# Attention step of a fused transformer kernel: transposes ahead of scores on TensorE, low halves ahead of the maximum on VectorE

## Chip, core and metric

The kernel runs on one core of one Trainium2 chip. The metric is the device time of one execution in microseconds (us), as the median of several runs. TensorE multiplies matrices and transposes, VectorE and ScalarE work on the results in PSUM, GpSimd works in SBUF, and SyncE issues the DMAs. Each engine takes its instructions in the order in which they are written; engines meet at semaphores.

## What is computed

The reference is a block of three parts on x of 4 x 1024 x 256: a mixture-of-experts feed-forward, attention with a small MLP, and the same feed-forward again. The attention, on which the change bears, is:

```python
q = (_ln(x, lnq_s, lnq_b) @ Wq + bq).reshape(Bq, Sq, H, HD).transpose(0, 2, 1, 3)   # k, v alike; H=16, HD=64
scores = jnp.einsum('bhqd,bhkd->bhqk', q, k) / SMAX
mask = jnp.triu(jnp.full((Sq, Sq), -999.0, dtype=scores.dtype), k=Sq - 1)
p = jax.nn.softmax(scores + mask, axis=-1)
att = jnp.einsum('bhqk,bhkd->bhqd', p, v).transpose(0, 2, 1, 3).reshape(Bq, Sq, AHD)
h = att @ Wo + bo + x
...
x = x + 0.5 * _L0_ffn_ref(_layernorm(x, axis=-1), ...)
x = x + _L0_attn_ref(_layernorm(x, axis=-1), ...)
x = x + 0.5 * _L0_ffn_ref(_layernorm(x, axis=-1), ...)
```

Here Sq is 1024, so that each of 4 batches and 16 heads has a 1024 x 1024 matrix of scores.

## The kernel before

Each engine has one hand-written stream for each phase: feed-forward, attention, MLP with the second feed-forward. Nothing reorders it: the code's order is the engine's order. In the names of the profile, `f_` belongs to the first feed-forward, `a_` to attention, `m_` and `g_` to what follows.

Attention is a loop of 512 steps. A step k takes 128 queries of one head against all 1024 keys. Eight steps (QT) make a head, 16 (STEPS) a pair of heads, 32 (ITER) one iteration of the loop (NIT = 16 iterations). The first iteration (`first`) is written out, the next ones but the last run as a hardware loop, and a last piece (`last`) of eight steps drains what is left. Matrices whose product needs more precision are kept as a high half (rounded to the matmul's type) and a low half (the rest), in two slots of one tile. What a step holds:

- TensorE (`on_tensor`, PE): scores of step k into `a_sc` (4 matmuls of 512 columns, line 1586; two buffers, so that the write waits for the exponential of step k-2); transposes of the probabilities of step k-3 (LAG = 3) into `a_tr` (8 of 128 columns, line 1598; two parts of four, one bank each; each part waits until the low half of the same part of the step before is taken); values of an earlier block into `a_ov` (4 matmuls, line 1622); and in some steps a projection piece of a coming pair into `a_pj` (lines 1541 and 1550).
- VectorE (`on_vector`, DVE): in every fourth step half of a finished block (`a_half`, line 1489); in every eighth one element of mask (line 1495); the negated maximum of each row of scores (`a_nmax`, line 1498); the reciprocal of the sum of the step before (`a_rden`, line 1503); and the low halves of the transposes in two parts (`a_pT`, line 1509), each of which waits for ScalarE's high half of that part.
- ScalarE (`on_scalar`, ACT): in every fourth step the other half of the finished block (`a_ao`, line 1334); the high halves of the transposes, two parts (`a_pT`, line 1341); the exponential of the scores of step k with its row sum (`a_pr`, line 1347; the sum is fetched by a short instruction of its own, ACTIVATION_READ_ACCUMULATOR), which waits for the maximum of step k; and after it the copy of a projection piece out of PSUM (`a_staged`, lines 1302 and 1299).
- GpSimd (`on_gpsimd`, POOL): multiplies the probabilities of the step before by `a_rden` (line 1425), and splits projection pieces into halves (lines 1378 to 1404).

Which steps have a projection piece stands in a table (`PLAN`, and `PLAN_FIRST` for the first iteration); QK pieces leave ScalarE by line 1302, V pieces by line 1299. In an iteration of the hardware loop 8 steps have a QK piece and 4 a V piece; the first iteration has 8 and 7, the last 4 and none. So in the steps 3 to 511 there are 124 QK pieces and 61 V pieces, 63 steps with a mask, and 126 steps with a finished block (steps 11, 15, ..., 511).

Of the kernel before, what the change touches and what calls it, by code (L numbers as in the profile page):

```python
# [20 lines left out]
F32 = mybir.dt.float32  # L21
F32R = mybir.dt.float32r
U32 = mybir.dt.uint32
ALU = mybir.AluOpType
# [3 lines left out]
P = 128  # L28
# [986 lines left out]
def attention_phase(nc, turns, tag, w, zT, w_split, bias, att):  # L1015
# [12 lines left out]
    ITER = 2 * STEPS  # L1028
    NIT = B * PAIRS // 2
    LAG = 3  # L1030
    QT = S // P
    NP = 4
# [7 lines left out]
    ident, bsb = kept["ident"], kept["bias"]  # L1040
# [11 lines left out]
    pT = m.sb("pT", [P, 2, 2, QT, BT], F32R, room=rooms.wide)  # L1052
    pr = m.sb("pr", [P, NP, S], room=rooms.rows)
# [4 lines left out]
    tr = m.ps("tr", [P, 2, BT], 2)  # L1058
# [3 lines left out]
    s = {n: m.sem(n) for n in (  # L1062
        "z_in wqk_in wv_in v_in k_dup sc masked negmax exp rden normed tr tr_hi tr_lo "
        "pj staged head0_hi head1_hi head0_lo v_hi first_split split pv half ov_read att att_out").split()}
# [60 lines left out]
    def transposes_at(k, first, last):  # L1125
        return not (first and k < LAG) and not (last and k >= LAG)
# [338 lines left out]
    def on_vector(dve, ahead):  # L1465
        rest = whole.ffn["vector"](dve)

        for n, (kind, part) in enumerate(FIRST):
            if kind != "V":
                xs, hi, lo = parts_of(kind, part, n % 2, 0)  # L1470
                for x in range(2):
                    dve.wait_ge(s["head%d_hi" % x], n + 1)
                    dve.tensor_tensor(lo[x], xs[x], hi[x].bitcast(F32), ALU.subtract)\
                        .then_inc(s["first_split" if x else "head0_lo"], 1)

        def body(it, first, last):
            for k in steps(last):
                u = it * ITER + k
                v = finished_at(k, first)
                if v:  # L1480
                    _, vhead, blk, _ = v
                    dve.wait_ge(s["pv"], it * BLOCKS + blk + 1)
                    if blk % 4 == 0 and not (first and blk < 4):

                        dve.wait_ge(s["att"], it * 2 + blk // 4)
                    if blk == 0 and first:

                        dve.wait_ge(f["res_out"], NB * 16 + 16)
                    dve.tensor_copy(half[rows_of_head(vhead), blk % 2], ov[rows_of_head(1 - vhead)])\  # L1489
                        .then_inc(s["half"], 1)  # L1490
                if not last:
                    dve.wait_ge(s["sc"], u + 1)
                    if k % QT == 0:

                        dve.tensor_scalar(sc[0:1, k % 2, S - 1:S], sc[0:1, k % 2, S - 1:S], MASK, None,
                                          ALU.add).then_inc(s["masked"], 1)
                        dve.wait_ge(s["masked"], it * (ITER // QT) + k // QT + 1)
                    dve.tensor_reduce(nmax[:, k % NP:k % NP + 1], sc[:, k % 2], AX.X, ALU.max,  # L1498
                                      negate=True).then_inc(s["negmax"], 1)
                if (k == 0 and not first) or (k > 0 and not last):  # L1500
                    j = (k - 1) % NP
                    dve.wait_ge(s["exp"], u)
                    dve.reciprocal(rden[:, j:j + 1], den[:, j:j + 1]).then_inc(s["rden"], 1)  # L1503
                if transposes_at(k, first, last):
                    t = (k - LAG) % ITER
                    for part in range(2):
                        dve.wait_ge(s["tr_hi"], 2 * (u - LAG) + part + 1)
                        to = pT[:, (t // 4) % 2, :, 4 * part:4 * part + 4, (t % 4) * P:(t % 4 + 1) * P]
                        dve.tensor_tensor(to[:, 1], tr[:, part].rearrange("p (t q) -> p t q", t=4),  # L1509
                                          to[:, 0].bitcast(F32), ALU.subtract).then_inc(s["tr_lo"], 1)  # L1510
                if ends(it) and k == STEPS + 6:
                    ahead["b1"]()
                if last and 2 < k < 5:
                    ahead["att_lo"](k - 3)
                if first and k == 1:
                    rest["z_stats"]()
                if first and k == 3:
                    rest["zz_stats"]()
                if first and k == 4:
                    rest["bias"](ov)  # L1520
                if first and k in (5, 6):
                    rest["zt_lo"](k - 5, ov[:])
        over_iterations(dve, body)

    def on_tensor(pe, ahead):
# [37 lines left out]
        def body(it, first, last):  # L1563
            for k in steps(last):
                u = it * ITER + k
                slot, head, tile = k // STEPS, (k // QT) % 2, k % QT
                if not last:

                    if k % STEPS == 0:

                        pe.wait_ge(s["k_dup"], it * 64 + slot * 32 + 64)
                        if slot:
                            pe.wait_ge(s["split"], before(it, STEPS))
                        elif not first:
                            pe.wait_ge(s["split"], before(it, 0) - 3)
                        else:
                            pe.wait_ge(s["first_split"], 3)
                            pe.wait_ge(f["res"], NB * 2)
                    if first and k == 4:
                        pe.wait_ge(s["first_split"], 4)  # L1580
                    if not (first and k < 2):

                        pe.wait_ge(s["exp"], u - 1)
                    for kb in range(S // BT):
                        for a in range(2):
                            o = pe.matmul(sc[:, k % 2, kb * BT:(kb + 1) * BT],  # L1586
                                          q_s[:, slot, head, tile * P:(tile + 1) * P],
                                          k_s[:, slot, head, a, kb * BT:(kb + 1) * BT],
                                          start=(a == 0), stop=(a == 1))
                    o.then_inc(s["sc"], 1)  # L1590
                if transposes_at(k, first, last):
                    pe.wait_ge(s["normed"], u - LAG + 1)
                    for part in range(2):
                        if not (first and k == LAG):

                            pe.wait_ge(s["tr_lo"], 2 * (u - LAG) + part - 1)
                        for j in range(4):
                            o = pe.transpose(tr[:, part, j * P:(j + 1) * P],  # L1598
                                             pr[:, (k - LAG) % NP, (4 * part + j) * P:(4 * part + j + 1) * P], ident[:])
                        o.then_inc(s["tr"], 1)  # L1600
                v = values_at(k, first)
                if v and not (last and v[2] >= 0):
                    vslot, vhead, blk, q = v
# [562 lines left out]
```

## Time and profile before

| | us |
|---|---|
| median of 3 runs | 2459.19 |
| lowest, highest | 2451.25, 2463.77 |
| the profiled execution | 2457.1 |
| its span, first to last instruction | 2454.2 |
| first scores of attention to last, in the trace | 298 to 1982 |

The profile gives for each engine its busy time, then the chain that ended last, then groups of instructions with their busy time, the mean time of one, and the idle time of the engine ahead of them with what ended it. In a timeline a row is one instruction or a run of the same kind: its start, its busy time and, in brackets, how long the engine sat idle before it and for whom. Of two rows of one engine the difference of the starts is the pace at which it takes them; a matmul's own duration reaches over the start of the next, because matmuls are pipelined. The granted clock (PEclk) is the share of TensorE's 2.4 GHz that it had in a stretch: 1.00 is 2.4 GHz, 0.50 is 1.2 GHz.

### The profile page before, as it was taken

How to read it: one execution, taken by the hardware profiler on the slowest of the kernel's cores; microseconds unless marked ns; L12 is line 12 of the kernel's file. 1: busy time of each engine (PE TensorE's matmuls, PEld its weight loads, DVE VectorE, ACT ScalarE, POOL GpSimd, SP SyncE). 2: the span in 40 equal slices, each digit the busy share in tenths (PEclk: the TensorE clock that was granted, in tenths of full speed). 3: DMA queues.
4: the chain of work that ended last, by engine and by line, in shares of the span. 5: the costliest groups of instructions: out<-in, count | busy, mean ns of one | idle time of the engine just before them, and what ended most of it. 6: DMA issues, size and time to landing. Idle time of an engine off the chain costs nothing.

```text
span 2454.2 us, 46643 instructions
## 1 busy us (share of the span) xinstructions
PE 2405.0 (98%) x14568; PEld 2087.9 (85%) x14568; DVE 1862.3 (76%) x3599; ACT 1686.6 (69%) x2920; POOL 1505.2 (61%) x1536
## 2 busy tenths in 40 slices
PE   8999889999999999999999999999999999999999
PEld 7888778888888888888888888888888879988888
DVE  7777677878878788887878878788887865556665
ACT  4555577878778787777878778787877864543333
POOL 1333277787777777767777777777768754542220
PEclk9999999999999999999999999999999999999999
DMA  5422531223212132221213312132221345331111
GB/s 204 172 102 94 181 112 44 87 68 96 95 40 89 45 101 71 75 95 43 86 60 100 97 35 94 43 98 73 77 95 43 108 169 171 122 130 34 46 51 43
DMA packets 128311, 220.16 MB, mean 90 GB/s; under 512 B 6810, under 2 KB 89652, under 8 KB 119476
## 3 DMA queue, kind: packets, MB, share of 16 engines
q1 hardware_dynamic: 128180, 218.78, 27.6%
q8 instruction: 37, 0.61, 0.1%
q14 instruction: 94, 0.77, 0.1%
HBM read 114.95 MB, written 53.48 MB: 69 GB/s over the span
## 4 chain that ended last, share of the span: by engine, by line
PE 81%; DVE 8%; issue 6%; POOL 2%; ACT 2%; DMA 1%; SPq 0%; DVEq 0%; ACTq 0%; POOLq 0%
PE a_ov L1622 19%; PE a_sc L1586 18%; PE a_tr L1598 18%; PE a_pj L1541 7%; PE a_pj L1550 4%; PE g_acc L896 3%; PE g_hid L855 3%; PE f_acc L896 3%; PE f_hid L855 2%; PE m_proj L2025 1%; POOL m_zin L1877 1%; PE m_hid L2091 1%; DVE f_hp L676 1%; DVE g_hp L676 1%; PE g_aux L832 1%
## 5 line engine op out<-in xcount | busy, mean ns | idle before, releaser
L1498 DVE TENSOR_REDUCE a_nmax<-a_sc 128x1 f32<-128x1024 f32 x512 | 626.8, 1224 | 260.3 <-PE a_sc L1586 252.1
L1425 POOL TENSOR_SCALAR a_pr<-a_pr,a_rden 128x1024 f32<-128x1024 f32 x512 | 575.1, 1125 | 256.2 <-DVE a_rden L1503 185.7
L1341 ACT ACTIVATE a_pT<-a_tr 128x512 fp32r<-128x512 f32 x1024 | 559.8, 596 | 205.5 <-PE a_tr L1598 197.2
L1509 DVE TENSOR_TENSOR a_pT<-a_tr,a_pT 128x512 fp32r<-128x512 f32 x1024 | 650.1, 677 | 17.7 <-ACT a_pT L1341 17.7
L1622 PE MATMUL a_ov<-a_pT,a_v_s 128*128 128x512 f32 x2048 | 600.2, 415 | 3.1 <-DVE a_half L1489 2.0
L1347 ACT ACTIVATE a_pr<-a_sc,a_nmax 128x1024 f32<-128x1024 f32 x512 | 573.5, 1120 | 31.8 <-DVE a_nmax L1498 28.2
L1586 PE MATMUL a_sc<-a_k_s,a_q_s 128*128 128x512 f32 x2048 | 554.1, 392 | 3.4 <-DMA a_k_s<-a_k_s 3.4
L1598 PEld LDWEIGHTS a_tr<-f_ident,a_pr 128*128 128x128 f32 x4096 | 473.0, 140 | 93.6 <-DVE a_pT L1509 18.8
L1598 PE MATMUL a_tr<-f_ident,a_pr 128*128 128x128 f32 x4096 | 537.8, 273 | 9.8 <-DVE a_pT L1509 9.6
L1586 PEld LDWEIGHTS a_sc<-a_k_s,a_q_s 128*128 128x128 f32 x2048 | 380.0, 188 | 83.7 <-DMA a_k_s<-a_k_s 3.6
L1622 PEld LDWEIGHTS a_ov<-a_pT,a_v_s 128*128 128x128 f32 x2048 | 347.5, 189 | 54.3 <-issue 4.9
L1541 PE MATMUL a_pj<-a_z_s,a_wqk_s 128*128 128x512 f32 x756 | 193.6, 391 | 2.5 <-issue 2.2
L1541 PEld LDWEIGHTS a_pj<-a_z_s,a_wqk_s 128*128 128x128 f32 x756 | 141.6, 188 | 34.9 <-issue 3.3
L1302 ACT ACTIVATE a_staged<-a_pj,f_bias 128x512 f32<-128x512 f32 x126 | 86.8, 689 | 93.8 <-PE a_pj L1541 77.4
L469 ACT ACTIVATE g_act_out<-g_hid,f_b 128x512 f32<-128x512 f32 x72 | 49.6, 688 | 144.5 <-PE g_hid L855 144.5
L896 PEld LDWEIGHTS f_acc<-f_w2p,f_hp 128*128 128x128 f32 x864 | 114.0, 193 | 11.1 <-DVE f_hp L676 6.3
L469 ACT ACTIVATE f_act_out<-f_hid,f_b 128x512 f32<-128x512 f32 x72 | 49.2, 684 | 107.0 <-PE f_hid L855 107.0
L896 PE MATMUL f_acc<-f_w2p,f_hp 128*128 128x256 f32 x864 | 117.5, 286 | 4.5 <-DVE f_hp L676 3.9
L896 PEld LDWEIGHTS g_acc<-g_w2p,g_hp 128*128 128x128 f32 x864 | 112.1, 190 | 8.2 <-DVE g_hp L676 2.9
L896 PE MATMUL g_acc<-g_w2p,g_hp 128*128 128x256 f32 x864 | 115.5, 283 | 1.3 <-DVE g_hp L676 0.9
L855 PE MATMUL f_hid<-f_xT,f_w1p 128*128 128x512 f32 x432 | 115.7, 404 | 0.0
L855 PE MATMUL g_hid<-g_xT,g_w1p 128*128 128x512 f32 x432 | 113.1, 397 | 0.0
(222 smaller groups left out, 3260.0 us busy)
## 6 DMA issues: line engine op xcount, KB each, us to landing
a_z_s<-zT SPq DMA_DIRECT2D x32, 1024.0 KB, 7.8
a_k_s<-a_k_s SPq DMA_DIRECT2D x62, 512.0 KB, 5.7
a_wqk_s<-w_split SPq DMA_DIRECT2D x64, 256.0 KB, 3.2
a_v_s<-a_v_b SPq DMA_DIRECT2D x16, 1024.0 KB, 4.6
att<-a_ao SPq DMA_DIRECT2D x32, 512.0 KB, 2.9
m_in<-att SPq DMA_DIRECT2D x16, 1024.0 KB, 6.1
a_wv_s<-w_split SPq DMA_DIRECT2D x17, 512.0 KB, 3.8
zT<-f_zT SPq DMA_DIRECT2D x8, 1024.0 KB, 3.9
```

The lines of the kernel that those rows point to most:

```text
L469: act.activation(act_out[:, e % 3], hid[:, (par + e) % 2], ACT.Gelu, bias=b1[:, weights_of(e):weights_of(e) + 1]).then_inc(s["gelu"], 1)
L855: o = pe.matmul(hid[:, (par + e) % 2], w1p[:, a, (c * NE + x) * HID:(c * NE + x + 1) * HID], xT[:, par, c, b], start=(n == 0), stop=(n == 5))
L896: o = pe.matmul(acc[:, t], hp[:, e % 3, a, t * P:(t + 1) * P], w2p[:, b, x * D:(x + 1) * D], start=False, stop=(e == NE - 1 and (a, b) == ...
L1341: act.activation(pT[:, (u // 4) % 2, 0, 4 * part:4 * part + 4, (u % 4) * P:(u % 4 + 1) * P], tr[:, part].rearrange("p (t q) -> p t q", t=4 ...
L1347: act.activation(pr[:, k % NP], sc[:, k % 2], ACT.Exp, bias=nmax[:, k % NP:k % NP + 1], accum_out=den[:, k % NP:k % NP + 1]).then_inc(s["e ...
L1425: pool.tensor_scalar(pr[:, k % NP], pr[:, k % NP], rden[:, k % NP:k % NP + 1], 1.0, ALU.mult, ALU.mult).then_inc(s["normed"], 1)
L1498: dve.tensor_reduce(nmax[:, k % NP:k % NP + 1], sc[:, k % 2], AX.X, ALU.max, negate=True).then_inc(s["negmax"], 1)
L1509: dve.tensor_tensor(to[:, 1], tr[:, part].rearrange("p (t q) -> p t q", t=4), to[:, 0].bitcast(F32), ALU.subtract).then_inc(s["tr_lo"], 1)
L1541: o = pe.matmul(bank[:], wqk_s[:, "QK".index(kind), c, a], z_s[:, c * 2 + b, part], start=(i == 0), stop=(i == 5))
L1586: o = pe.matmul(sc[:, k % 2, kb * BT:(kb + 1) * BT], q_s[:, slot, head, tile * P:(tile + 1) * P], k_s[:, slot, head, a, kb * BT:(kb + 1) * ...
L1598: o = pe.transpose(tr[:, part, j * P:(j + 1) * P], pr[:, (k - LAG) % NP, (4 * part + j) * P:(4 * part + j + 1) * P], ident[:])
L1622: o = pe.matmul(ov[:], v_s[:, vslot, kt, 2 * vhead:2 * vhead + 2] .rearrange("p k f -> p (k f)"), pT[:, blk % 2, a, kt], start=(kt == 0 an ...
```

## The change

Two blocks of code move within a step; nothing is added or taken away, and ScalarE's, GpSimd's and SyncE's streams stay as they are. On TensorE the transposes of step k-3 come ahead of the scores of step k. On VectorE the low halves of those transposes come ahead of the mask, the maximum and the reciprocal, behind `a_half`.

```diff
@@ on_vector
                     dve.tensor_copy(half[rows_of_head(vhead), blk % 2], ov[rows_of_head(1 - vhead)])\
                         .then_inc(s["half"], 1)
+                if transposes_at(k, first, last):
+                    t = (k - LAG) % ITER
+                    for part in range(2):
+                        dve.wait_ge(s["tr_hi"], 2 * (u - LAG) + part + 1)
+                        to = pT[:, (t // 4) % 2, :, 4 * part:4 * part + 4, (t % 4) * P:(t % 4 + 1) * P]
+                        dve.tensor_tensor(to[:, 1], tr[:, part].rearrange("p (t q) -> p t q", t=4),
+                                          to[:, 0].bitcast(F32), ALU.subtract).then_inc(s["tr_lo"], 1)
                 if not last:
                     dve.wait_ge(s["sc"], u + 1)
...
                     dve.wait_ge(s["exp"], u)
                     dve.reciprocal(rden[:, j:j + 1], den[:, j:j + 1]).then_inc(s["rden"], 1)
-                if transposes_at(k, first, last):
...
@@ on_tensor
                 slot, head, tile = k // STEPS, (k // QT) % 2, k % QT
+                if transposes_at(k, first, last):
+                    pe.wait_ge(s["normed"], u - LAG + 1)
+                    for part in range(2):
+                        if not (first and k == LAG):
+
+                            pe.wait_ge(s["tr_lo"], 2 * (u - LAG) + part - 1)
+                        for j in range(4):
+                            o = pe.transpose(tr[:, part, j * P:(j + 1) * P],
+                                             pr[:, (k - LAG) % NP, (4 * part + j) * P:(4 * part + j + 1) * P], ident[:])
+                        o.then_inc(s["tr"], 1)
                 if not last:
...
                     o.then_inc(s["sc"], 1)
-                if transposes_at(k, first, last):
...
```

On VectorE, in steps 9 and 10 of the first iteration, this stood in a row before (`a_tr_hi` counts ScalarE's high halves, `a_sc` TensorE's scores, `a_exp` ScalarE's exponentials):

```order
L1498 TENSOR_REDUCE a_nmax<-a_sc 128x1 [waits a_sc]
L1503 RECIPROCAL a_rden<-a_den 128x1 [waits a_exp]
L1509 TENSOR_TENSOR a_pT<-a_tr,a_pT 128x4x128 [waits a_tr_hi] x2
L1498 TENSOR_REDUCE a_nmax<-a_sc 128x1 [waits a_sc]
L1503 RECIPROCAL a_rden<-a_den 128x1 [waits a_exp]
L1509 TENSOR_TENSOR a_pT<-a_tr,a_pT 128x4x128 [waits a_tr_hi] x2
```

The same steps on VectorE in the changed kernel:

```order
L1496 TENSOR_TENSOR a_pT<-a_tr,a_pT 128x4x128 [waits a_tr_hi] x2
L1505 TENSOR_REDUCE a_nmax<-a_sc 128x1 [waits a_sc]
L1510 RECIPROCAL a_rden<-a_den 128x1 [waits a_exp]
L1496 TENSOR_TENSOR a_pT<-a_tr,a_pT 128x4x128 [waits a_tr_hi] x2
L1505 TENSOR_REDUCE a_nmax<-a_sc 128x1 [waits a_sc]
L1510 RECIPROCAL a_rden<-a_den 128x1 [waits a_exp]
```

The low halves of a step now stand ahead of that step's maximum.

On ScalarE, in steps 7 to 9, the same rows stand in both kernels (`a_tr` counts TensorE's transposed parts, `a_negmax` VectorE's maxima):

```order
L1341 ACTIVATE a_pT<-a_tr 128x4x128 [waits a_tr] x2
L1347 ACTIVATE a_pr,a_den<-a_sc,a_nmax 128x1024 [waits a_negmax]
L1302 ACTIVATE a_staged<-a_pj,f_bias 128x512 [waits a_pj,a_split]
L1341 ACTIVATE a_pT<-a_tr 128x4x128 [waits a_tr] x2
L1347 ACTIVATE a_pr,a_den<-a_sc,a_nmax 128x1024 [waits a_negmax]
L1341 ACTIVATE a_pT<-a_tr 128x4x128 [waits a_tr] x2
```

Nothing moved there: a step's high halves stand behind the exponential of the step before.

On TensorE, in step 7, this stood in a row before:

```order
L1586 MATMUL a_sc<-a_k_s,a_q_s 128x512 [waits a_exp]
L1586 MATMUL a_sc<-a_k_s,a_q_s 128x512 x3
L1598 MATMUL a_tr<-f_ident,a_pr 128x128 [waits a_tr_lo,a_normed]
L1598 MATMUL a_tr<-f_ident,a_pr 128x128 x3
L1598 MATMUL a_tr<-f_ident,a_pr 128x128 [waits a_tr_lo]
L1598 MATMUL a_tr<-f_ident,a_pr 128x128 x3
```

The same step on TensorE in the changed kernel:

```order
L1574 MATMUL a_tr<-f_ident,a_pr 128x128 [waits a_tr_lo,a_normed]
L1574 MATMUL a_tr<-f_ident,a_pr 128x128 x3
L1574 MATMUL a_tr<-f_ident,a_pr 128x128 [waits a_tr_lo]
L1574 MATMUL a_tr<-f_ident,a_pr 128x128 x3
L1596 MATMUL a_sc<-a_k_s,a_q_s 128x512 [waits a_exp]
L1596 MATMUL a_sc<-a_k_s,a_q_s 128x512 x3
```

The transposes, with their waits for the low halves of the step before, now stand ahead of the scores.

## Rows read from the trace of the kernel before

**Rows 1.** The page: busy time of each engine, its share, instructions.

```profile
PE 2405.0 (98%) x14568; PEld 2087.9 (85%) x14568; DVE 1862.3 (76%) x3599; ACT 1686.6 (69%) x2920; POOL 1505.2 (61%) x1536
```

**Rows 2.** Waits between 400 and 1950 us: who for whom, total, times, longest.

```profile
DVE a_nmax L1498 <- PE a_sc L1586: 233.5, 221, 1.7
ACT a_pT L1341 <- PE a_tr L1598: 183.3, 325, 2.1
...
PEld a_tr L1598 <- DVE a_pT L1509: 18.8, 57, 1.1
...
PE a_tr L1598 <- DVE a_pT L1509: 5.7, 13, 0.7
```

**Rows 3.** Timeline of PE over two steps (start, busy time, what).

```profile
1202.46 1.08 PE L1586 MATMUL a_sc<-a_k_s,a_q_s 128*128 128x512 f32 x4
1203.38 1.03 PE L1598 MATMUL a_tr<-f_ident,a_pr 128*128 128x128 f32 x8
1204.17 1.17 PE L1622 MATMUL a_ov<-a_pT,a_v_s 128*128 128x512 f32 x4
1205.17 1.52 PE L1541 MATMUL a_pj<-a_z_s,a_wqk_s 128*128 128x512 f32 x6
1206.54 1.08 PE L1586 MATMUL a_sc<-a_k_s,a_q_s 128*128 128x512 f32 x4
```

**Rows 4.** Timeline of DVE over one step with a mask.

```profile
1199.71 1.27 DVE L1509 TENSOR_TENSOR a_pT<-a_tr,a_pT 128x512 fp32r<-128x512 f32 x2
1200.90 0.14 DVE L1495 TENSOR_SCALAR a_sc<-a_sc 1x1 f32<-1x1 f32 x1
1201.08 1.23 DVE L1498 TENSOR_REDUCE a_nmax<-a_sc 128x1 f32<-128x1024 f32 x1
```

**Rows 5.** Timeline of ACT: the exponential behind that maximum, and its sum.

```profile
1202.34 1.12 ACT L1347 ACTIVATE a_pr<-a_sc,a_nmax 128x1024 f32<-128x1024 f32 x1
1203.35 0.19 ACT L1347 ACTIVATION_READ_ACCUMULATOR a_pr<-a_sc,a_nmax 128x1 f32 x1
```

**Rows 6.** Timeline of ACT: high halves that follow a sum with nothing between.

```profile
627.42 0.21 ACT L1347 ACTIVATION_READ_ACCUMULATOR a_pr<-a_sc,a_nmax 128x1 f32 x1
627.53 1.20 ACT L1341 ACTIVATE a_pT<-a_tr 128x512 fp32r<-128x512 f32 x2
```

**Rows 7.** Timeline of ACT and DVE at the loop's end, and DVE's first low halves.

```profile
1980.34 0.21 ACT L1347 ACTIVATION_READ_ACCUMULATOR a_pr<-a_sc,a_nmax 128x1 f32 x1
1980.42 0.68 ACT L1334 ACTIVATE a_ao<-a_ov,f_bias 64x512 f32<-64x512 f32 x1
1981.09 1.09 ACT L1341 ACTIVATE a_pT<-a_tr 128x512 fp32r<-128x512 f32 x2
...
1983.86 1.14 ACT L1341 ACTIVATE a_pT<-a_tr 128x512 fp32r<-128x512 f32 x2 [0.23 <-PE a_tr L1598]
...
1984.49 0.69 DVE L1509 TENSOR_TENSOR a_pT<-a_tr,a_pT 128x512 fp32r<-128x512 f32 x1 [0.67 <-ACT a_pT L1341]
...
312.54 0.69 DVE L1509 TENSOR_TENSOR a_pT<-a_tr,a_pT 128x512 fp32r<-128x512 f32 x1 [2.09 <-ACT a_pT L1341]
```

**Rows 8.** Groups of attention, 700 to 1800 us: busy, mean ns of one | idle before.

```profile
L1302 ACT ACTIVATE a_staged<-a_pj,f_bias 128x512 f32<-128x512 f32 x83 | 57.2, 689 | 60.3 <-PE a_pj L1541 47.9 <-POOL a_k_s L1404 12.4
...
L1299 ACT ACTIVATE a_staged<-a_pj 128x512 f32<-128x512 f32 x44 | 26.3, 598 | 16.4 <-PE a_pj L1550 16.4
```

**Rows 9.** Stretches: length, busy time of each engine (instructions), granted clock, DMA share, GB/s.

```profile
269.20:272.60 3.40, 0.77 (x6) 0.69 (x6) 3.23 (x6) 3.05 (x6) 0.00 (x0) 1.00 1.10 366
272.60:276.00 3.40, 3.40 (x14) 3.01 (x13) 3.24 (x9) 0.42 (x1) 1.95 (x3) 0.50 1.01 353
312.80:326.40 13.60, 9.74 (x57) 6.97 (x57) 11.57 (x27) 11.40 (x23) 9.26 (x14) 1.00 0.45 150
1992.90:1996.30 3.40, 3.40 (x10) 2.62 (x9) 3.40 (x2) 0.00 (x0) 0.00 (x0) 0.50 0.27 43
```

**Rows 10.** Timeline of ACT in a step with a piece: its copy waits for PE.

```profile
1207.00 0.69 ACT L1302 ACTIVATE a_staged<-a_pj,f_bias 128x512 f32<-128x512 f32 x1 [0.80 <-PE a_pj L1541]
```

More of the change, by code:

```diff
@@ L1503, in body @@
                     dve.reciprocal(rden[:, j:j + 1], den[:, j:j + 1]).then_inc(s["rden"], 1)
-                if transposes_at(k, first, last):
[L1505 to L1510, printed above, removed]
                 if ends(it) and k == STEPS + 6:
@@ L1590, in body @@
                     o.then_inc(s["sc"], 1)
-                if transposes_at(k, first, last):
[L1592 to L1600, printed above, removed]
                 v = values_at(k, first)
```

## The prediction

> **What bounds the kernel now.** I read the busy times first: TensorE is busy for 98% of the span, all others for 76% or less [rows 1]. A busy share of matmuls whose ends are modelled proves little, so the timeline of PE comes next, by its starts [rows 3]: scores 1202.46 to 1203.38 (0.92 us), transposes to 1204.17 (0.79), values to 1205.17 (1.00), projection to 1206.54 (1.37), and the next scores stand right behind. A step without a projection piece is 2.71 us of PE, one with a piece 4.08. The waits say the same from the other side [rows 2]: VectorE waits for scores (233.5 us in 221 places) and ScalarE for transposes (183.3 in 325), while TensorE waits for low halves only 18.8 + 5.7 us. So PE sets the pace and the others have slack.
>
> How much slack is there for PE to gain? The attention loop, taken from ScalarE's first high halves (step 3) to the end of its last exponential, runs from 312.54 - 0.63 = 311.9 us to 1983.86 - 0.23 = 1983.6 us [rows 7], that is 1672 us for 509 steps, 3.28 each. PE's own work in it is 509 x 2.71 + 185 pieces x 1.37 = 1379 + 253 = 1632 us. No order of the same instructions can give back more than the 40 us between.
>
> **What the change does, part by part.** Nothing is added or removed: same instructions, same DMAs. Three queues matter.
>
> TensorE: the transposes pass the 4 matmuls of the scores. The seams stay three a step (a transpose behind a matmul, a matmul behind a transpose), so by the starts of [rows 3] the step's work stays 2.71 or 4.08. I cost the move at 0. What now stands behind the transposes' wait for `a_tr_lo` is the scores as well, which is the first danger: PE cannot make scores of step k before the low halves of the step before are taken.
>
> VectorE: the low halves pass mask, maximum and reciprocal. Its work is the same too. But the low halves wait for ScalarE's high halves, and now the maximum of the same step stands behind them.
>
> ScalarE: its order does not change, and that decides. It makes the high halves of a step behind the exponential of the step before. Follow one round in the changed order: high half (ScalarE) lets VectorE take the two low halves; behind these, by VectorE's order, comes the maximum of the same step; that lets ScalarE make the exponential; behind that, by ScalarE's order, come the high halves of the next step. This is a closed chain that goes once round in each step, and none of its members overlap. Before, the maximum stood ahead of the low halves, so the round went maximum, exponential, high half of the next step, low half, and then the maximum of the step after that: once round in two steps, with room for it.
>
> The round's length, by the starts of rows in which the second instruction waited for the first or stood right behind it:
> - first high half to first low half: 1983.86 to 1984.49, 0.63 us [rows 7] (the second high half ends before the second low half can start, so it costs nothing);
> - two low halves up to the next of VectorE's instructions: 1199.71 to 1200.90, 1.19 [rows 4];
> - maximum to exponential: 1201.08 to 1202.34, 1.26 [rows 4, 5];
> - exponential to the fetch of its sum: 1202.34 to 1203.35, 1.01 [rows 5];
> - that fetch to the next high half: 627.42 to 627.53, 0.11 [rows 6].
>
> Together 4.20 us a step. Some steps add to it, on the same two queues:
> - the mask, between low half and maximum: 1200.90 to 1201.08, 0.18 [rows 4], in 63 steps: 11 us;
> - the copy of a projection piece, between exponential and next high half: 0.69 us for QK, 0.60 for V [rows 8], 124 and 61 times: 86 + 37 = 122 us. Today these copies hide in ScalarE's slack;
> - the finished block `a_ao`, there too: from fetch to high half 1980.34 to 1981.09 = 0.75 [rows 7], less 0.11: 0.64, 126 times: 81 us. VectorE's `a_half` (ahead of the low halves) runs beside the exponential and costs nothing; without that cover it would be another such term.
>
> Sum: 509 x 4.20 = 2138, and 11 + 122 + 81 = 214, together **2352 us** for the stretch that takes 1672 now: **+680 us**. The first steps also hold work of the phase before on both engines; I leave it out of the sum and in the range.
>
> Do the others fit under this round? PE needs 1632 of 2352 us. In a step it has its projection done some 4.08 us after the transposes begin, and these can begin as soon as the low halves of the step before are read; from there ScalarE needs the maximum, the exponential and its sum (2.3 us), the high halves with VectorE's answer, and a second maximum and exponential before it asks for that piece: over 6 us. So the copy should not wait for PE any more, unlike today [rows 10]. GpSimd's normalising has three steps of lag and 1505 us of work in the whole kernel [rows 1]. I take both at 0; if PE were late for each of the 185 copies by as much as today's 0.80 us [rows 10], that is 148 us more.
>
> TensorE's clock is the other cost that is not in the sum. PE will be busy for some 1632 / 2352 = 69% of the loop, in idle pieces of about 1.5 us. At the head of attention there is a stretch like that: 9.74 of 13.60 us busy (72%), and the granted clock is 1.00, 2.4 GHz, all through [rows 9]. It fell to 0.50 behind a stretch with 0.77 of 3.40 us busy [rows 9], which the new order doesn't have. So I take no fall. At 0.50 the values' matmuls touch 10 in 3.40 us [rows 9], at most 0.43 us each; a step of PE is then 8 x 0.43 + 0.79 to 1.58 = 4.2 to 5.0 us, with a piece 2.6 more. That is hidden if it comes singly, and takes over the bound if it stays: 509 x 4.2 + 185 x 2.6 = 2619 us at least, +267 on the round.
>
> The Trainium skill speaks for such a fall (TensorE: Matmul & The Clock Gate, "A second HAM failure mode: psum-queue depth-cycling"): short idle times of the PE between groups of matmuls made the clock swing between its two levels, and the throughput fell though each matmul looked the same. By that rule the loop would give the third rival below. The trace of this case does not bear it out so far: the stretch at 72% has no swing [rows 9].
>
> **Rivals.**
> 1. **The round is not the bound: faster.** The two moves would shorten the way from scores to the freeing of `a_tr`, and PE's 18.8 + 5.7 us of waits for it would go [rows 2]: 2457 - 25 = about 2430, at the very best 2457 - 40 = 2417. It decides at the point where the round, with its extras, is below PE's 3.28 us a step. I get 2352 / 509 = 4.62. Every term was taken from rows where nothing else intervened, so 1.3 us would have to be wrong; this needs ScalarE to have its high halves done ahead of the exponential before, which its order excludes.
> 2. **PE comes late into the round.** Copies of pieces wait for PE by 0.80 us in 185 steps, because the values at a block's start wait for `a_ao` and `a_half` and push the projection back: 3137 + 148 = 3285.
> 3. **The clock stays low.** PE at 1.2 GHz becomes the bound: 3137 + 267 = 3400, and up to 3800 if the transposes slow as well.
> 4. **The pieces partly hide.** If half of the 122 + 81 us of extras fell into a wait that is there anyway, 3137 - 100 = 3037. ScalarE's order speaks against it: all of them stand in the round.
>
> **How the numbers follow.** The profiled execution took 2457.1 us, 3 outside its span and 2 below the median of 2459.2. 2457.1 + 680 = **3137 us** (against the median 3139, which changes nothing). Chances: the round as worked out 0.82, with its own range of 3090 to 3200 (0.1 us a step either way is 51 us, the first steps' extra work a few us up); rival 1, 0.03; rival 2, 0.08; rival 3, 0.03; rival 4, 0.04. The range that leaves two in ten out, taken a little up towards rival 2 because a hand-over that costs more is easier to miss than one that costs less: 3080 to 3240. A measurement of this kernel can tell 0.5% from no change. Faster by more: 0.03, all of rival 1; within 0.5%: 0.01; slower: 0.96.
>
> **What the profile of the changed kernel would show.** If the round is right: scores come every 4.2 us in plain steps, some 4.9 in steps with a copy or a block and 5.5 with both; in each step the starts read high half, low half, maximum, exponential, one behind the other; the maximum waits for nothing of its own (no wait for scores), VectorE's first low half waits for ScalarE in nearly all 509 steps, ScalarE's exponential for VectorE's maximum by some 2 us each time (from the end of the high halves, 1.1 us into the round, to 0.63 + 1.19 + 1.26 = 3.08; some 1000 us in all), and TensorE's transposes for `a_pT`'s low halves by hundreds of us. The copies of pieces wait for nobody. The busy times of all groups stay, PE's share of the span falls to 2405 / 3137 = 77%, and the clock is 1.00 throughout attention. Wrong would be: waits of VectorE for scores that are still there (rival 1), waits of `a_staged` for `a_pj` (rival 2), or 0.50 in the row of the granted clock (rival 3).

## The result

The changed kernel takes 3135.28 us (median of 4 runs), the kernel before 2457.49 us beside it; the ratio is 1.2754, with a 95% interval of 1.2711 to 1.2798. Forecast were 3137 us and a range of 3080 to 3240. One of the four runs took 3379 us at a mean granted clock of 0.67 where the others have 0.99; the ratio leaves it out, and the median of the other three is 3133.7. Differences below are taken from 3135.28. The profiled execution took 3132.6 us, its span is 3130.8.

The page's busy times of the changed kernel answer to [rows 1]:

```profile
PE 2566.3 (82%) x14568; PEld 2054.2 (66%) x14568; DVE 1870.1 (60%) x3599; ACT 1657.0 (53%) x2920; POOL 1501.0 (48%) x1536
```

The instructions are the same in number. VectorE, ScalarE and GpSimd are busy for within 2% of what they were. TensorE's busy time is 161 us higher with the same matmuls. A likely reason is how it is counted: in [rows 3] a row is busy for 0.15 to 0.24 us past the start of the next, and where the next has to wait, that piece is no longer covered by it. All shares fell, since the span grew by 677 us. Where the engines wait is in the waits between 400 and 2600 us, which answer to [rows 2] (who for whom, total, times, longest):

```profile
ACT a_pr L1347 <- DVE a_nmax L1505: 965.5, 477, 2.2
DVE a_pT L1496 <- ACT a_pT L1341: 915.5, 476, 3.6
POOL a_pr L1425 <- DVE a_rden L1510: 894.0, 477, 3.9
PEld a_tr L1574 <- DVE a_pT L1496: 491.3, 664, 2.4
PE a_tr L1574 <- DVE a_pT L1496: 314.0, 253, 2.0
PEld a_ov L1622 <- ACT a_ao L1334: 181.1, 98, 1.9
```

ScalarE waits for VectorE 477 times, once a step, and VectorE for ScalarE as often: two engines that wait for each other in turn. VectorE's waits for scores, 233.5 us in [rows 2], are gone from the list, and so are ScalarE's for transposes. Two groups over the whole span say the same, and that the maximum waits for almost nothing any more (busy, mean ns, idle before with its releaser):

```profile
L1347 ACT ACTIVATE a_pr<-a_sc,a_nmax 128x1024 f32<-128x1024 f32 x512 | 571.1, 1115 | 1040.3 <-DVE a_nmax L1505 1040.3
...
L1505 DVE TENSOR_REDUCE a_nmax<-a_sc 128x1 f32<-128x1024 f32 x512 | 622.5, 1216 | 5.3 <-PE a_sc L1596 3.1
```

One round of it, in the timelines of ACT and of DVE (start, busy time, what, idle before), a step with a projection piece and the plain one behind it:

```profile
1206.38 1.12 ACT L1347 ACTIVATE a_pr<-a_sc,a_nmax 128x1024 f32<-128x1024 f32 x1 [2.00 <-DVE a_nmax L1505]
1207.39 0.19 ACT L1347 ACTIVATION_READ_ACCUMULATOR a_pr<-a_sc,a_nmax 128x1 f32 x1
1207.48 0.68 ACT L1302 ACTIVATE a_staged<-a_pj,f_bias 128x512 f32<-128x512 f32 x1
1208.05 1.08 ACT L1341 ACTIVATE a_pT<-a_tr 128x512 fp32r<-128x512 f32 x2
1211.14 1.12 ACT L1347 ACTIVATE a_pr<-a_sc,a_nmax 128x1024 f32<-128x1024 f32 x1 [2.00 <-DVE a_nmax L1505]
1212.15 0.19 ACT L1347 ACTIVATION_READ_ACCUMULATOR a_pr<-a_sc,a_nmax 128x1 f32 x1
1212.24 1.07 ACT L1341 ACTIVATE a_pT<-a_tr 128x512 fp32r<-128x512 f32 x2
```

```profile
1208.68 1.29 DVE L1496 TENSOR_TENSOR a_pT<-a_tr,a_pT 128x512 fp32r<-128x512 f32 x2 [2.27 <-ACT a_pT L1341]
1209.89 1.22 DVE L1505 TENSOR_REDUCE a_nmax<-a_sc 128x1 f32<-128x1024 f32 x1
...
1212.86 1.29 DVE L1496 TENSOR_TENSOR a_pT<-a_tr,a_pT 128x512 fp32r<-128x512 f32 x2 [1.69 <-ACT a_pT L1341]
```

Follow the starts: high half 1208.05, low half 1208.68 (0.63), maximum 1209.89 (1.21), exponential 1211.14 (1.25), its sum 1212.15 (1.01), next high half 1212.24 (0.09). That is 4.19 us, and 1208.68 to 1212.86 on VectorE is 4.18, where the forecast had 4.20. The copy of the projection piece stands openly between 1207.48 and 1208.05 and takes 0.57 us of the round.

The granted clock was 1.00 over the loop (length, busy times of PE, PEld, DVE, ACT, POOL, clock, DMA):

```profile
400.00:2600.00 2200.00, 1712.74 (x9052) 1293.98 (x9050) 1277.36 (x2085) 1217.69 (x2204) 1183.19 (x1221) 1.00 0.18 55
```

### The profile page after: what moved, and what is told of

The parts are those of the page before. It is cut to its first block, busy times and chain, and to the rows that moved or that the text cites. A ratio compares the mean times of both kernels' runs of the same rounds, so it can differ in the third digit from the quotient of the medians.

```text
span 3130.8 us, 46643 instructions
## 1 busy us (share of the span) xinstructions
PE 2566.3 (82%) x14568; PEld 2054.2 (66%) x14568; DVE 1870.1 (60%) x3599; ACT 1657.0 (53%) x2920; POOL 1501.0 (48%) x1536
## 4 chain that ended last, share of the span: by engine, by line
issue 30%; DVE 30%; ACT 20%; PE 15%; ACTq 2%; DMA 1%; DVEq 1%; POOL 0%; SPq 0%; POOLq 0%
DVE a_nmax L1505 20%; ACT a_pT L1341 8%; ACT a_pr L1347 5%; DVE a_pT L1496 4%; ACT a_ao L1334 3%; ACT a_staged L1302 2%; PE m_proj L2025 2%; PE g_acc L896 2%; PE g_hid L855 2%; PE f_acc L896 2%; PE f_hid L855 2%; PE m_hid L2091 1%; PE m_acc L2062 1%; ACT a_staged L1299 1%; ACTq L1339 1%
## 5 line engine op out<-in xcount | busy, mean ns | idle before, releaser
L1496 DVE TENSOR_TENSOR a_pT<-a_tr,a_pT 128x512 fp32r<-128x512 f32 x1024 | 659.8, 686 | 978.9 <-ACT a_pT L1341 978.9
L1347 ACT ACTIVATE a_pr<-a_sc,a_nmax 128x1024 f32<-128x1024 f32 x512 | 571.1, 1115 | 1040.3 <-DVE a_nmax L1505 1040.3
L1574 PE MATMUL a_tr<-f_ident,a_pr 128*128 128x128 f32 x4096 | 614.8, 284 | 340.2 <-DVE a_pT L1496 339.1
L1574 PEld LDWEIGHTS a_tr<-f_ident,a_pr 128*128 128x128 f32 x4096 | 440.4, 141 | 574.1 <-DVE a_pT L1496 491.3
L1622 PE MATMUL a_ov<-a_pT,a_v_s 128*128 128x512 f32 x2048 | 569.3, 400 | 186.1 <-ACT a_ao L1334 182.8
L1596 PE MATMUL a_sc<-a_k_s,a_q_s 128*128 128x512 f32 x2048 | 606.2, 418 | 3.4 <-DMA a_k_s<-a_k_s 3.4
L1622 PEld LDWEIGHTS a_ov<-a_pT,a_v_s 128*128 128x128 f32 x2048 | 377.2, 189 | 320.0 <-ACT a_ao L1334 181.1
L1341 ACT ACTIVATE a_pT<-a_tr 128x512 fp32r<-128x512 f32 x1024 | 551.7, 595 | 16.3 <-issue 14.8
L1596 PEld LDWEIGHTS a_sc<-a_k_s,a_q_s 128*128 128x128 f32 x2048 | 350.4, 191 | 46.6 <-DMA a_k_s<-a_k_s 3.6
L1550 PEld LDWEIGHTS a_pj<-a_wv_s,a_z_s 128*128 128x128 f32 x768 | 100.8, 191 | 6.3 <-issue 0.7
```

What stands on the lines that cost most here:

```text
L1341: act.activation(pT[:, (u // 4) % 2, 0, 4 * part:4 * part + 4, (u % 4) * P:(u % 4 + 1) * P], tr[:, part].rearrange("p (t q) -> p t q", t=4 ...
L1347: act.activation(pr[:, k % NP], sc[:, k % 2], ACT.Exp, bias=nmax[:, k % NP:k % NP + 1], accum_out=den[:, k % NP:k % NP + 1]).then_inc(s["e ...
L1550: o = pe.matmul(bank[:, t * 2 * P:(t + 1) * 2 * P], z_s[:, c * 2 + a, part // 2, col:col + P], wv_s[:, c, b], start=(i == 0), stop=(i == 5))
L1574: o = pe.transpose(tr[:, part, j * P:(j + 1) * P], pr[:, (k - LAG) % NP, (4 * part + j) * P:(4 * part + j + 1) * P], ident[:])
L1596: o = pe.matmul(sc[:, k % 2, kb * BT:(kb + 1) * BT], q_s[:, slot, head, tile * P:(tile + 1) * P], k_s[:, slot, head, a, kb * BT:(kb + 1) * ...
L1622: o = pe.matmul(ov[:], v_s[:, vslot, kt, 2 * vhead:2 * vhead + 2] .rearrange("p k f -> p (k f)"), pT[:, blk % 2, a, kt], start=(kt == 0 an ...
```

## The experiments

All times below are medians of runs beside the kernel before on the same chip, which took 2457 to 2460 us there; ratios are to it.

### Which of the two moves costs the time

The first kernel takes VectorE's move alone (the first hunk of the change), the second TensorE's alone (the second hunk).

```diff
@@ dve_only, on_vector
+                if transposes_at(k, first, last):
+                    ...
                 if not last:
                     dve.wait_ge(s["sc"], u + 1)
...
-                if transposes_at(k, first, last):
-                    ...
```

> VectorE's move alone (low halves ahead of mask, maximum and reciprocal); TensorE's order as before. Theory 1 (the loss is the round high half, low half, maximum, exponential of ScalarE and VectorE, in which TensorE has no part): the round is the same 4.18 us a plain step, so 3135 us, within 40. Theory 2 (the loss comes from the scores now standing behind the transposes' wait on TensorE): the scores are back in front, so most of the loss goes, under 2700 us.

Measured: 3225.9 us, ratio 1.312 (1.3092 to 1.3148). VectorE's move alone brings the whole loss, so theory 2 falls. But it is 91 us more than both moves together, twice what I had allowed; the last group of experiments is about that.

```diff
@@ pe_only, on_tensor
+                if transposes_at(k, first, last):
+                    pe.wait_ge(s["normed"], u - LAG + 1)
+                    ...
                 if not last:
...
                     o.then_inc(s["sc"], 1)
-                if transposes_at(k, first, last):
-                    ...
```

> TensorE's move alone (transposes ahead of scores); VectorE's order as before. I expect a second, smaller round that was hidden behind the first: the second part of the transposes waits for the second low half of the step before, scores follow, then maximum, reciprocal, low halves. By starts in the traces: two low halves 1.27, four transposes 0.44, scores to maximum 1.11, maximum to low halves 1.21: 4.03 us a step, with wake-ups some 4.1, the same in steps with a projection piece since TensorE's own work is 4.08 there. 509 x 4.1 + 12 for masks = 2099 against 1672 in the loop of before: 2457 + 427 = 2880 us, 2830 to 2950. Theory 2 (all of the loss is TensorE's move): 3135. If TensorE's move costs nothing, as the sum of the prediction had it: 2457.

Measured: 2916.19 us, ratio 1.1861 (1.1832 to 1.189). TensorE's move is not free either: alone it costs 456 us, by a round of its own that the prediction did not have. In its timelines of PE and DVE:

```profile
1206.16 1.25 PE L1574 MATMUL a_tr<-f_ident,a_pr 128*128 128x128 f32 x8 [1.26 <-DVE a_pT L1509]
1207.17 1.17 PE L1596 MATMUL a_sc<-a_k_s,a_q_s 128*128 128x512 f32 x4
...
1208.38 1.23 DVE L1498 TENSOR_REDUCE a_nmax<-a_sc 128x1 f32<-128x1024 f32 x1 [1.67 <-PE a_sc L1596]
1209.52 0.15 DVE L1503 RECIPROCAL a_rden<-a_den 128x1 f32<-128x1 f32 x1
1209.59 1.27 DVE L1509 TENSOR_TENSOR a_pT<-a_tr,a_pT 128x512 fp32r<-128x512 f32 x2
...
1212.54 1.22 DVE L1498 TENSOR_REDUCE a_nmax<-a_sc 128x1 f32<-128x1024 f32 x1 [1.68 <-PE a_sc L1596]
```

Transposes wait for the low halves of the step before (1.26 us), scores stand behind them, the maximum waits for the scores (1.67 us), and the low halves stand behind the maximum. From maximum to maximum it is 1208.38 to 1212.54 = 4.16 us, where I had put 4.1. In ScalarE's timeline from 400 to 1900 us nearly all steps take this 4.16, those with a finished block or a QK piece too, since ScalarE's extra copies are not in this round. With both moves the low halves no longer stand behind the maximum, so this round is open and the other one is closed: the two moves trade one round for another.

### Is the maximum in these rounds, and TensorE in the first?

Half of the maximum's columns are left out, in the changed kernel, in the kernel before and in the one with TensorE's move alone; and half of the matmuls of the scores, in the changed kernel and in the one before.

```diff
@@ after_half_max, before_half_max, pe_only_half_max
-                    dve.tensor_reduce(nmax[:, k % NP:k % NP + 1], sc[:, k % 2], AX.X, ALU.max,
+                    dve.tensor_reduce(nmax[:, k % NP:k % NP + 1], sc[:, k % 2, :BT], AX.X, ALU.max,
...
-                    act.activation(pr[:, k % NP], sc[:, k % 2], ACT.Exp, bias=nmax[:, k % NP:k % NP + 1],
+                    act.activation(pr[:, k % NP], sc[:, k % 2], ACT.Exp, bias=nmax[:, k % NP:k % NP + 1], scale=0.8,
@@ after_pe_light, before_pe_light
-                        for a in range(2):
+                        for a in range(1):
                             o = pe.matmul(sc[:, k % 2, kb * BT:(kb + 1) * BT],
...
-                                          start=(a == 0), stop=(a == 1))
+                                          start=True, stop=True)
```

> The changed kernel, leaving out half of the columns of the maximum (and with the scores scaled by 0.8 in the exponential so that it stays finite): VectorE's instruction falls from 1.22 to about 0.69 us. Theory 1: the maximum lies in the round, so the loop falls by 0.53 us in each of 512 steps, 271 us: 2864 us, within 25. If VectorE has slack that matters (it is busy for 60% of the span) the gain is much smaller.

Measured: 2864.55 us, 271 us less than the changed kernel: every one of the 512 x 0.53 us comes through. A plain step takes 3.65 us instead of 4.18, and the exponential's own time is as before (1117 ns against 1115), so the scaling brought nothing of it.

> The kernel before with half of the columns of the maximum left out (and the same scale in the exponential). VectorE is off the path there, so 2457 us, at most 25 less (TensorE's few waits for low halves).

Measured: 2454.54 us, ratio 0.999 (0.9976 to 1.0004). The same 271 us of VectorE's work taken from the kernel before bring nothing. This pair shows that the maximum was hidden and is now on the path.

> TensorE's move alone, leaving out half of the columns of the maximum (and the scores scaled by 0.8 in the exponential so that it stays finite). If its 4.16 us a step are a round through scores, maximum and low halves, plain steps fall by the maximum's 0.53 us, while the 184 steps with a projection piece stay at TensorE's own 4.08: 324 x 0.53 + 184 x 0.08 = 186 us less than 2916, so 2730 us, within 30. If TensorE alone set the 4.16: 2916.

Measured: 2736.87 us, 179 less than TensorE's move alone (forecast: 186 less). So that second round also runs through the maximum: plain steps fall to 3.62 us, and steps with a QK piece stay at 4.08, where TensorE's own work takes over.

> The changed kernel, leaving out the low part of the scores (2 of 4 matmuls, 0.46 us of TensorE a step, 235 us in all). Theory 1: TensorE is off the path of the loop, so 3135 us, at most 20 less. Theory 2: scores come 0.46 us earlier in each of 512 steps, 235 us less: 2900 us.

Measured: 3163.04 us, ratio 1.2854 (1.2825 to 1.2883). Theory 2 falls: 235 us of TensorE's work less give no gain, and plain steps are still at 4.18 us. But it is 28 us slower, which neither theory had. A stretch of 500 us of this kernel, and the same stretch of the changed one:

```profile
500.00:1000.00 500.00, 374.91 (x1806) 280.93 (x1805) 286.24 (x468) 273.79 (x493) 260.61 (x268) 0.89 0.17 53
```

```profile
500.00:1000.00 500.00, 388.68 (x2045) 292.59 (x2045) 290.60 (x474) 276.70 (x501) 265.61 (x272) 1.00 0.17 53
```

With less to do TensorE had a lower granted clock, 0.89 on average against 1.00, and VectorE and ScalarE did fewer instructions in the same time. Where the 28 us lie, ScalarE's waits between 400 and 2600 us tell, and one turn of the hardware loop (it comes once in 32 steps) in the timelines of PE and ACT:

```profile
ACT a_pT L1341 <- issue: 27.0, 13, 2.3
ACT a_staged L1299 <- PE a_pj L1550: 11.7, 28, 0.5
```

```profile
1193.12 2.73 PE L1550 MATMUL a_pj<-a_wv_s,a_z_s 128*128 128x256 f32 x12
1195.68 1.05 PE L1574 MATMUL a_tr<-f_ident,a_pr 128*128 128x128 f32 x8
...
1195.89 0.60 ACT L1299 ACTIVATE a_staged<-a_pj 128x512 f32<-128x512 f32 x1 [0.52 <-PE a_pj L1550]
1198.47 1.08 ACT L1341 ACTIVATE a_pT<-a_tr 128x512 fp32r<-128x512 f32 x2 [1.98 <-issue]
```

At a granted clock of 0.50 to 0.58 (1192 to 1196 us) the V piece takes 2.56 us by the starts, against 1.43 in the changed kernel, and its copy waits for it. Behind this late copy ScalarE's pause at the turn (its wait for "issue") is 2.0 us and more; in the changed kernel it is 1.0 to 1.3 us, 14.8 us in all. The two rows make 11.7 + 12.2 = 24 of the 28 us. The longer pause goes with the late copy and not with the clock alone: the kernel before with the same matmuls left out has it too, 26.9 us in 13 places, at a clock of 1.00, and there V copies wait for TensorE as well (22.8 us in 59 places). Why the pause has this length stays open.

> The kernel before, leaving out the low part of the scores (2 of 4 matmuls, 0.46 us of TensorE a step). TensorE sets the pace there, so the time falls, until VectorE is the bound (some 2.8 us in steps with a mask or a block): by 130 to 235 us, to 2220 to 2330 us. No change would say that TensorE was not the bound before.

Measured: 2404.01 us, ratio 0.9786 (0.976 to 0.9811). The sign is right, TensorE was the bound, but only 53 us of 235 come, less than the 130 that I gave at least. The waits of that kernel between 400 and 1900 us name what is late next (PEld is TensorE's loading of weights):

```profile
PEld a_tr L1598 <- DVE a_pT L1509: 143.6, 277, 1.9
...
PE a_tr L1598 <- POOL a_pr L1425: 61.4, 100, 1.6
```

TensorE's weight loads wait for VectorE's low halves, 143.6 us against 18.8 in [rows 2], and its matmuls for GpSimd's normalising, for which the kernel before had no wait in its list. So both stood close behind TensorE. Which of them takes back how much of the 235 us was not tried.

### Does cutting the round at ScalarE give the time back?

ScalarE makes the high halves of step k+1 ahead of the exponential of step k, in the changed kernel and in the kernel before; then also the copy of the finished block.

```diff
@@ act_early, before_act_early, on_scalar
-                if transposes_at(k, first, last):
+                n = k + 1
+                if transposes_at(n, first, last) if n < ITER else not last:
                     for part in range(2):
-                        act.wait_ge(s["tr"], 2 * tile + part + 1)
-                        u = (k - LAG) % ITER
+                        act.wait_ge(s["tr"], 2 * (tile + 1) + part + 1)
+                        u = (n - LAG) % ITER
@@ act_ahead, as well: from the head of the step to behind these high halves
-                v = finished_at(k, first)
+                v = finished_at(n, first) if n < ITER else None if last else finished_at(0, False)
                 if v:
...
```

> The changed kernel, with ScalarE's high halves of step k+1 ahead of the exponential of step k, so that the round of theory 1 is cut at ScalarE. Theory 1: plain steps fall from 4.18 to about 2.7 us, TensorE's own work; a part stays at the ends of blocks, since TensorE's values wait there for ScalarE's copy of the block before, which now stands between an exponential and high halves that wait for TensorE's transposes: some 1.7 us in 128 places, 220 us. About 2690 us, 2600 to 2780. If the round is not the cause: near 3135.

Measured: 2734.76 us, ratio 1.1115 (1.1092 to 1.1137). 400 of the 678 us are back, with every instruction kept. Its waits between 400 and 2600 us show where the rest went:

```profile
ACT a_pT L1342 <- PE a_tr L1575: 624.6, 367, 3.3
DVE a_pT L1497 <- ACT a_pT L1342: 545.4, 376, 3.7
...
PE a_ov L1623 <- ACT a_ao L1334: 194.3, 123, 2.9
```

TensorE waits for the block's copy 123 times, as forecast. But ScalarE waits for transposes for 624.6 us, where [rows 2] had 183.3: of the plain steps only about one in four takes the 2.7 us that I had put, most take 3.2 to 4.1 (exponential to exponential, 400 to 1900 us). The total fell in the range all the same; that plain steps would still be this slow, the forecast did not have.

> The changed kernel with ScalarE's high halves of step k+1 and its copy of a finished block (that of step k+1) both ahead of the exponential of step k. If the 277 us that the version with early high halves alone still lost lie in TensorE's wait for the block's copy (172 us and more in that trace), most of them go: about 2600 us, 2550 to 2650. If they lie elsewhere: 2735.

Measured: 2615.14 us, ratio 1.063 (1.0595 to 1.0665): another 120 us. The remaining 158 us against the kernel before I didn't take apart; exponentials now stand behind instructions that wait for TensorE, and ScalarE's wait for transposes is still 496.6 us (398 times) there.

> The kernel before, with ScalarE's high halves of step k+1 ahead of the exponential of step k. In the old order of TensorE the transposes of step k+1 stand behind the scores of step k+1, so the exponential of step k now waits for scores, transposes and high halves of the next step, and the scores of step k+2 wait for that exponential: a round of its own of some 3.8 us in plain steps. About 3000 us, 2800 to 3100. If an early high half were good in itself, 2430.

Measured: 3279.34 us, ratio 1.3362 (1.3325 to 1.34). The same edit that gave 400 us to the changed kernel costs the kernel before 822 us. Its waits between 400 and 2600 us show the forecast round:

```profile
ACT a_pT L1342 <- PE a_tr L1599: 1052.8, 463, 5.7
...
PE a_sc L1587 <- ACT a_pr L1348: 217.6, 238, 1.1
```

ScalarE waits in each step for the transposes, which stand behind the scores, and the scores wait for ScalarE's exponential. Its size was missed (3000 forecast, 3100 the upper end). Plain steps take 3.9 to 4.2 us and steps with a piece 3.9, near the 3.8 of the forecast, but those with a finished block 6.6 to 8.7 (exponential to exponential, 400 to 1900 us): I had no term for the block ends, where ScalarE's order also holds the block's copy. The granted clock was lower here too, 0.92 from 400 to 2600 us; what this adds was not taken apart.

### Why VectorE's move alone is slower than both

In the trace of the kernel with VectorE's move alone TensorE has this (timeline of PE, then its stretches around it: length, busy times of PE, PEld, DVE, ACT, POOL, granted clock, DMA):

```profile
1267.70 1.25 PE L1598 MATMUL a_tr<-f_ident,a_pr 128*128 128x128 f32 x8 [0.60 <-DVE a_pT L1496]
1271.24 1.87 PE L1622 MATMUL a_ov<-a_pT,a_v_s 128*128 128x512 f32 x4 [2.28 <-ACT a_ao L1334]
1272.90 1.91 PE L1586 MATMUL a_sc<-a_k_s,a_q_s 128*128 128x512 f32 x4
1274.61 1.19 PE L1598 MATMUL a_tr<-f_ident,a_pr 128*128 128x128 f32 x8
1275.55 1.16 PE L1622 MATMUL a_ov<-a_pT,a_v_s 128*128 128x512 f32 x4
```

```profile
1268.00:1271.40 3.40, 1.12 (x9) 0.70 (x8) 2.14 (x4) 1.99 (x4) 1.67 (x2) 1.00 0.00 0
1271.40:1274.80 3.40, 3.40 (x9) 2.55 (x10) 2.49 (x4) 1.39 (x3) 2.41 (x3) 0.51 0.00 0
```

At a block's start scores and transposes are both done, and TensorE idles for 2.28 us until ScalarE has copied the block before. Behind that the clock is at 0.51, its lower level of 1.2 GHz: values take 1.66 us by the starts (1271.24 to 1272.90) instead of 1.00 in [rows 3], scores 1.71 instead of 0.92, transposes 0.94 instead of 0.79. Where a projection piece follows, TensorE is then late for ScalarE's next high halves. Between 400 and 2600 us ScalarE waits for transposes like this:

```profile
ACT a_pT L1341 <- PE a_tr L1598: 67.1, 59, 2.2
```

With 12.8 us of waits for pieces that is 80 us in which ScalarE waits for TensorE, of the 91 to be explained. In the changed kernel there are no such waits, and the transposes of a step wait as well, which spreads TensorE's idle time over two places; that this keeps its clock up was not tested. Over the loop the clock is 0.90 in the one and 1.00 in the other:

```profile
400.00:2600.00 2200.00, 1791.26 (x8725) 1402.64 (x8724) 1229.76 (x2006) 1187.74 (x2123) 1145.41 (x1182) 0.90 0.17 51
```

To try this I gave TensorE more work in that place:

```diff
@@ dve_only_filled, on_tensor
                     if q == 0:

+                        if not (first or last or ends(it) and k >= STEPS):
+                            pe.wait_ge(s["staged"], before(it, k))
+                            for _ in range(6):
+                                pe.matmul(pj[:], q_s[:, slot, head, tile * P:(tile + 1) * P],
+                                          k_s[:, slot, head, 0, :BT], start=True, stop=True)
                         pe.wait_ge(s["tr_lo"], 2 * (u - LAG))
```

> The kernel with VectorE's move alone, and 6 more matmuls of 512 columns on TensorE (1.4 us, into the projection's bank, their result unused) ahead of the values of each block's start, where TensorE otherwise idles for 2.3 us until ScalarE has copied the block before. Theory A (the 90 us by which VectorE's move alone was slower than both moves come from the granted clock, which falls to 1.2 GHz behind that idle time and makes TensorE late for the next transposes): the clock stays at 1.00 and the time falls to about 3140 us, within 30, although TensorE has more work. Theory B (the scores ahead of the transposes make these late whatever the clock): no gain, 3225 us or more.

Measured: 3140.51 us, ratio 1.2757 (1.2713 to 1.2801), 85 us less than without the useless matmuls, and level with both moves together. Its clock over the loop:

```profile
400.00:2600.00 2200.00, 1890.56 (x9736) 1412.85 (x9736) 1273.72 (x2078) 1215.05 (x2197) 1183.75 (x1222) 1.00 0.18 54
```

ScalarE's waits for TensorE have fallen to 5.5 us. The added instructions can only delay TensorE, and the order is as it was; so theory A holds, and B falls.

## Why the prediction was right, point by point

- **TensorE was the bound, and no order could gain more than 40 us.** The first half held: with less work on TensorE the kernel before got faster, with less on VectorE it didn't. That it was the bound by little was not seen; of 235 us only 53 came. The 40 us are a subtraction that no run tried.
- **A closed round of 4.20 us a step, found by following the waits through the fixed orders of ScalarE and VectorE.** Held: 4.18 us, and each of its five terms within 0.02 us. Halving one member took its full 0.53 us x 512; cutting the round in one place gave 400 us back.
- **The extras.** Each was somewhat wrong, and the errors nearly cancel. Pieces were too dear: a QK piece takes 0.57 us of the round and a V piece 0.48, where I had 0.69 and 0.60. I had taken a copy's duration, but the next instruction starts before its end; the gap of the starts is the price. That is some 22 us too much for 185 pieces, and 10 more for the 0.02 us by which the round itself was too long. Blocks were too cheap. They come in two kinds, two of one and two of the other in turn, about half each. In ScalarE's timeline of the changed kernel, one of the dear kind, one of the cheap kind, and the turn of the hardware loop:

```profile
1202.37 0.19 ACT L1347 ACTIVATION_READ_ACCUMULATOR a_pr<-a_sc,a_nmax 128x1 f32 x1
1202.59 0.68 ACT L1334 ACTIVATE a_ao<-a_ov,f_bias 64x512 f32<-64x512 f32 x1
1203.30 1.09 ACT L1341 ACTIVATE a_pT<-a_tr 128x512 fp32r<-128x512 f32 x2
...
1626.51 0.19 ACT L1347 ACTIVATION_READ_ACCUMULATOR a_pr<-a_sc,a_nmax 128x1 f32 x1
1626.60 0.67 ACT L1334 ACTIVATE a_ao<-a_ov,f_bias 64x512 f32<-64x512 f32 x1
1627.17 1.06 ACT L1341 ACTIVATE a_pT<-a_tr 128x512 fp32r<-128x512 f32 x2
...
1631.35 0.59 ACT L1299 ACTIVATE a_staged<-a_pj 128x512 f32<-128x512 f32 x1
1632.96 1.08 ACT L1341 ACTIVATE a_pT<-a_tr 128x512 fp32r<-128x512 f32 x2 [1.02 <-issue]
```

  The first takes 0.93 us from the sum's fetch to the high half, less 0.09 that is 0.84; the second 0.66, so 0.57. The mean is 0.70, where I had 0.64 from a single block: 8 us too little in 126 of them. Why there are two kinds was not looked into. A term was missing as well: at the turn of the loop ScalarE stood for 1.0 to 1.3 us with nothing to wait for in the profile, 13 times. A step with such a turn takes 6.10 us on average, against 4.86 for its V piece and mask alone, so 16 us in all. Together 2352 - 10 - 22 + 8 + 16 = 2344 us, and the stretch took 2349 in the trace (312.33 to 2661.16 us); the 5 us left may be the first steps' other work, which I had left to the range, but were not taken apart. So the round was forecast, and that 3137 came within 2 us of 3135 was luck.
- **TensorE's move at 0.** The step that was right only by company. With VectorE's move it costs nothing, and even spares 91 us; alone it costs 456, by the round through scores and maximum. I had named the scores behind the transposes' wait as the first danger and then not followed it to the end.
- **No fall of the clock.** Held for this kernel (1.00 from 400 to 2600 us), and not by much: in three of its nearest relatives the clock did fall, with TensorE's old order (0.90, some 85 of the 91 us), with less work on TensorE (0.89, 28 us slower) and in the kernel before with early high halves (0.92). The price of the low clock was about right as well: 1.66 and 1.71 us for four matmuls of 512 columns, where 4 x 0.43 = 1.72 was the bound. The rule of the Trainium skill (TensorE: Matmul & The Clock Gate, "A second HAM failure mode: psum-queue depth-cycling") that short idle times between groups of matmuls make the clock swing was borne out in those three, but not in the changed kernel. What the prediction took from it as well, that each matmul looked the same, is not so here: four of the values took 1.66 us instead of 1.00.
- **Rival 2** (TensorE late for the copies of pieces) is absent from the waits; something near it happened, by way of the clock, with VectorE's move alone, mostly as high halves that wait for transposes, and with TensorE's lighter scores, as V copies that wait. **Rivals 1 and 4** found no support. PE's share was forecast at 77% and is 82% on the page; the prediction took its busy time to stay, and it rose by 161 us.

## What to carry to other kernels

Before an instruction is moved in a fixed order, draw the waits of one step together with each engine's order and look for a closed way; its length divided by the steps that it spans is a floor for the pace, whatever the engines' busy shares say. Moving an instruction can leave every duration as it is and turn a way that closes in two steps into one that closes in one, and then all the small copies that used to hide stand in it. Two moves that look like one idea should be costed alone as well as together, since each can close or open a way of its own. And a total that comes out right does not say that its terms are: check them one by one in the new trace.

## What was not expected of the hardware

TensorE with less to do made the kernel slower: leaving out 235 us of matmuls cost 28 us, with a granted clock of 0.89 on average against 1.00. Six useless matmuls ahead of each block's values gained 85 us, and the clock went from 0.90 back to 1.00. In the rows shown, the low clock came behind an idle time of 2.28 us, in a loop in which TensorE was busy for 81% of the time by the profile (1791 of 2200 us); in the changed kernel with lighter scores it fell to 0.72 from 1188 to 1190 us, behind an idle time of 2.02 us. In the changed kernel itself, with waits of TensorE of up to 2.0 us, it stayed at 1.00, so the length of one idle time does not settle it here. And the turn of a hardware loop cost ScalarE 1.0 to 1.3 us in the changed kernel and 2.0 us and more where the copy ahead of it had come late.
